# A megakernel of FFN, latent attention and FFN: moving the stages' transfers from SyncE's queue to ScalarE's

## The reference

```python
x = x + 0.5 * ffn(layernorm(x))        # x @ W.T + b, plus top-2 of 8 gated LoRA experts of rank 16
x = x + attention(layernorm(x))        # 16 heads, causal, 1024 tokens
x = x + 0.5 * ffn(layernorm(x))

# attention(x)
kv = rmsnorm(x @ W_kv) * g_kv          # rank 64
qc = x @ W_q                           # rank 128
q  = [qc @ W_qdec, rope(qc @ W_qrope)] # 16 + 32 columns a head
k  = [kv @ W_kdec, rope(x @ W_krope)]
out = softmax(causal(q @ k.T / sqrt(48))) @ (kv @ W_vdec) @ W_o
```

## Time and profile before

| what | value |
|---|---|
| median of three | 1967.87 us |
| the profiled execution | 1969.61 us, span 1967.9 us |
| PE busy | 1883.3 us, 96% of the span |
| DVE, ACT, POOL busy | 1428.7, 1017.2, 854.4 us |
| mean granted TensorE clock | 0.978 |
| moved by DMA | 307.60 MB, mean 156 GB/s |

### The profile page before, as it was taken

One profiled execution on the slowest core, in us unless ns is written; L12 is line 12 of the kernel. 1 busy time (PEld: TensorE's weight loads), 2 busy tenths in 40 slices (PEclk: granted clock), 3 DMA queues, 4 the chain that ended last, 5 costly groups with the idle time before them and its releaser, 6 DMA issues.

```text
span 1967.9 us, 32231 instructions
## 1 busy us (share of the span) xinstructions
PE 1883.3 (96%) x10832; PEld 1313.5 (67%) x10832; DVE 1428.7 (73%) x4570; ACT 1017.2 (52%) x2125; POOL 854.4 (43%) x912
## 2 busy tenths in 40 slices
PE   6789999999999999999999999999999999999994
PEld 5446666767776676767767777667767677677653
DVE  5667777777777787777877777777777778677622
ACT  3335555555555555555554555555555545555550
POOL 3456454443545445355443545444453544522121
PEclk9789999999999999999999999999999999999997
DMA  3675675676775667666675676656677666665511
GB/s 103 190 184 158 164 191 152 155 186 167 172 178 131 177 155 184 167 159 158 162 177 146 162 199 158 158 156 161 159 175 192 152 146 178 174 154 121 113 33 46
DMA packets 169813, 307.60 MB, mean 156 GB/s; under 512 B 15088, under 2 KB 33776, under 8 KB 169648
## 3 DMA queue, kind: packets, MB, share of 16 engines
q1 hardware_dynamic: 169648, 305.53, 61.7%
HBM read 179.12 MB, written 126.35 MB: 155 GB/s over the span
## 4 chain that ended last, share of the span: by engine, by line
PE 81%; DVE 7%; DMA 6%; ACT 2%; issue 2%; POOL 1%; SPq 1%; POOLq 0%; DVEq 0%
PE mx_b L788 14%; PE st_b L756 14%; PE st_b L758 12%; PE o_b L776 12%; PE tp_b L824 5%; DMA st<-k_scratch 4%; PE tp_b L821 4%; PE wj_b L713 4%; PE wj_b L700 3%; PE wj_b L682 3%; PE wj_b L693 2%; PE wj_b L715 2%; DVE mx_b L975 1%; PE wj_b L722 1%; PE wj_b L728 1%
## 5 line engine op out<-in xcount | busy, mean ns | idle before, releaser
L861 ACT ACTIVATE probs<-st_b 128x512 f32<-128x512 f32 (+3 forms) x1536 | 700.4, 489 | 569.3 <-PE st_b L758 519.5
L975 DVE CUSTOM_DVE_ANT_0 mx_b<-mx_b,tri 128x256 f32<-128x256 f32 (+3 forms) x1024 | 511.0, 515 | 118.9 <-PE mx_b L788 114.7
L756 PE MATMUL st_b<-st 97*128 97x512 f32 (+2 forms) x1536 | 578.7, 381 | 7.1 <-ACT probs L861 4.7
L788 PE MATMUL mx_b<-st 96*128 96x256 f32 (+2 forms) x1536 | 554.3, 406 | 19.2 <-DVE mx_s L975 8.1
L758 PE MATMUL st_b<-st,k_st 96*128 96x512 f32 (+2 forms) x1536 | 531.8, 350 | 0.0
L978 DVE TENSOR_REDUCE mx_s<-mx_b 128x1 f32<-128x512 f32 (+1 forms) x512 | 333.8, 652 | 137.3 <-PE mx_b L788 132.0
L788 PEld LDWEIGHTS mx_b<-st 96*128 96x128 f32 x1536 | 279.6, 192 | 203.7 <-issue 107.3
L1176 POOL TENSOR_SCALAR_AFFINE_SELECT probs<-probs 128x512 f32<-128x512 f32 x256 | 166.7, 658 | 529.7 <-ACT probs L861 529.7
L756 PEld LDWEIGHTS st_b<-st 97*128 97x128 f32 x1536 | 291.9, 190 | 105.5 <-ACT probs L861 39.8
L758 PEld LDWEIGHTS st_b<-st,k_st 96*128 96x128 f32 x1536 | 294.2, 192 | 30.1 <-issue 9.1
L776 PE MATMUL o_b<-probs,v_s 128*17 128x512 f32 (+3 forms) x3072 | 287.2, 492 | 0.9 <-POOL probs L1176 0.9
(11 more groups left out here) (192 smaller groups left out, 2281.6 us busy)
## 6 DMA issues: line engine op xcount, KB each, us to landing
st<-q_scratch SPq DMA_DIRECT2D x128, 384.0 KB, 5.8
st<-k_scratch SPq DMA_DIRECT2D x128, 384.0 KB, 8.6
k_st<-k_scratch SPq DMA_DIRECT2D x128, 384.0 KB, 8.7
q_scratch<-hi_t SPq DMA_DIRECT2D x32, 768.0 KB, 4.3
q_scratch<-lo_t SPq DMA_DIRECT2D x32, 768.0 KB, 5.3
k_scratch<-hi_t SPq DMA_DIRECT2D x30, 768.0 KB, 6.2
k_scratch<-lo_t SPq DMA_DIRECT2D x30, 768.0 KB, 4.8
ao_scratch<-o_f SPq DMA_DIRECT2D x256, 32.0 KB, 1.9
```

What stands on the lines that cost most here:

```text
L756: nc.tensor.matmul(dst, k1_st[u][0:SHIFT + 1, a, P * j:P * j + P], q_st[u][0:SHIFT + 1, a, q0:q0 + w], start=True, stop=False)
L788: nc.tensor.matmul(mx_b[:, m % 2, 0:w], q_st[u][0:SHIFT, a, P * i:P * i + P], k1_st[u][0:SHIFT, a, k0:k0 + w], start=True, stop=True).then ...
L861: nc.scalar.activation(probs[:, a, PLACE[s]:PLACE[s] + n], st_b[:, a % 2, HALF - n:HALF], ACT.Exp, scale=SCALE).then_inc(exp_done, 1)
L975: nc.vector.tensor_tensor_reduce(src, src, tri[:, HALF - n:HALF], 1.0, NEG, ALU.add, ALU.max, dst).then_inc(mx_done, 1)
```

## The change

ACT's queue now issues the stages' transfers (letters D and d, 80 steps with the same waits as before), the eleven weight transfers, and the stores of the high parts (u, 64). SP keeps the stores of the low parts (u, 64), the stacks, the shift rows and the attention output: 384 letters. All five order strings are new; PE, DVE and POOL have the same letters as before in another order, and ACT has 144 more.

```diff
-SP_STEPS = {JOB_A: ("x_load", "x_store"), JOB_C: ("x_load", "ao_load", "x_store")}
+LOADS = {JOB_A: ("x_load", "x_store"), JOB_C: ("x_load", "ao_load", "x_store")}
     "ACT": {
+        "D": [(name, n) for n in range(NJ) if LANE[n] == 0 for name in LOADS[JOBS[n][0]]],
+        "d": [(name, n) for n in range(NJ) if LANE[n] == 1 for name in LOADS[JOBS[n][0]]],
+        "u": [("store", n, 0) for n in range(NU)],
     "SP": {
-        "u": [("store", n, hl) for n in range(NU) for hl in range(2)],
+        "u": [("store", n, 1) for n in range(NU)],
-        "J": [(name, n) for n in range(NJ) if LANE[n] == 0 for name in SP_STEPS[JOBS[n][0]]],
-        "j": [(name, n) for n in range(NJ) if LANE[n] == 1 for name in SP_STEPS[JOBS[n][0]]],
@@ scalar
+                elif name == "x_load":
+                    if done:
+                        act.wait_ge(own.stored, 16 * done)
+                        if JOBS[own_last][0] == JOB_A:
+                            act.wait_ge(own.normed[1], count(own_last, 1) + 1)
...
+                    nc.scalar.dma_start(own.xa[:, :, :], x_g[k] if kind == JOB_A else x1_d[k]).then_inc(own.x_in, 16)
+                    if n == 0:
+                        load_first()
+                    elif n == 1:
+                        load_attention()
+                elif name == "ao_load":
...
+                elif name == "x_store":
+                    act.wait_ge(own.wj_free, bank_use(n, "y1") + 1)
+                    nc.scalar.dma_start(x1_d[k] if kind == JOB_A else out_g[k], own.xa[:, :, :]).then_inc(own.stored, 16)
+                elif name == "store":
+                    act.wait_ge(hic_done, n + 1)
+                    act.wait_ge(hir_done, n + 1)
+                    scratch_free(act, n)
+                    nc.scalar.dma_start(scratch_rows(n, 0), hl_t[SPARE[n]][0][:, :, :].bitcast(F32)).then_inc(
+                        hl_out[SPARE[n]][0], 16)
```

`scratch_free` and `scratch_rows` are new names for lines 616 to 621 before, unchanged. The strings, cut to their heads (whole ones have 3892, 2107 or 2251, and 528 or 384 letters):

```diff
 PE
-"JJJJPPPPjjjjJJJjjjJJJJPjjPjPJjPPPPPJPJJjPJPPXXPXPXXXPXXJXPXJXXPJXXPXXPFPXXXXXXXXXPXXPJXJXXSSXXSSXXSSPXXS..."
+"JJJJPPPPjjjjJJJjjjJJJJPjjPjPJjPPPPPJPJJjPJPPXXPPXXXPXXPXXJPXXJXXPJXXPXPXXXXXXXXXFXPXXJJPXXXXXXXXXXSXSXPX..."
 ACT
-"BJJJJwwwwwCCCJCjjjjJjjJJJJCjjCjCJjCHCCHCCJCJJjCJJCHCHCCCJCCBCCHCCCEEEEEEHEEEEECCEECEEEHCCCJJJEEEHEJCEECE..."
+"DBdJJJJwwwwwCCCJCjjjjJjjDDdJJJJCjjCjCJjCHCuCHuCCJCJJjCJJCHCuHuCCCCJCBCDCHuCCDCHEEuECEECEECEEEEEEEEHEuCCC..."
 SP
-"JjJJjuuuuquuuukqqsusuquukJuusJasssuuuuqksusqauksusuaJJqkususqakuussauuqkuqsaksusJsuuaqkJJsqsakssuuaqkuuJ..."
+"uuqkuuqqqsuskuussassuqkuqsksaussuaqkuqskasussauqkusqsakussaqkusqskaussaqkuqsaksussaqkqsksuassaqkuqsksuas..."
```

More of the change, by code:

```diff
@@ L238 @@
+        "MnJMMJMMoMMoMoMoMJMJJJJJMMJMMfJMJnJMMoMoMoMMoJMMJMMMMMMMMMMMMMMMJMMJMMJMMJfJnMMMMJMMJMMoMMooMoMMMJJJJJMM"
+        "JMMfJMnMJJoJMMoMoMMoJMMJMMMMMMMMMMMMMMMMMMMMMfnMMMMMMMoooMMoMMMMMMMfnMMMMMooMoMMoMMMMMMMMMMMMMMMMMMMMMMM"
         "MfnooooooooJJJJJJJJJJJJJJJJJJJoooojjjjjjjjjjjjjjjjjjj",
@@ L530, in rope, with scratch_free, scratch_rows @@
             engine.tensor_tensor(r[:, 1, :], r[:, 1, :], r[:, 0, :], ALU.add).then_inc(roped[SPARE[n]], 1)
+        def scratch_free(engine, n):
+            m, pair, side = UNIT[n]
+            b, half = divmod(m, 2)
+            if b > 1:
+                g = NQ * (b - 2) + NQ // NP * (pair + 1) - 1
+                engine.wait_ge(qk_in[g % 2][half], 64 * (g // 2 + 1))
+                engine.wait_ge(k2_in[half], 32 * (g + 1))
+        def scratch_rows(n, hl):
+            m, pair, side = UNIT[n]
+            b, half = divmod(m, 2)
+            rows = qk_d[side][b % 2, hl, PH * DQ * pair:PH * DQ * (pair + 1), HALF * half:HALF * (half + 1)]
+            return rows.rearrange("(r x) t -> r x t", x=3)
         def landed(sp, g, half):
@@ L562, in _ @@
-            for name, n, *arg in walk("SP"):
-                if name == "x_load":
-                    kind, k = JOBS[n]
-                    own = lanes[LANE[n]]
-                    done = IN_LANE[n]
-                    if done:
-                        own_last = max(i for i in range(n) if LANE[i] == LANE[n])
-                        sp.wait_ge(own.stored, 16 * done)
-                        if JOBS[own_last][0] == JOB_A:
-                            sp.wait_ge(own.normed[1], count(own_last, 1) + 1)
-                    if kind == JOB_C:
-                        before = JOB_OF[JOB_A, k]
-                        sp.wait_ge(lanes[LANE[before]].stored, 16 * (IN_LANE[before] + 1))
-                    if done and LANE[n]:
-                        sp.wait_ge(pv_done, NV * QUADS)
-                    sp.dma_start(own.xa[:, :, :], x_g[k] if kind == JOB_A else x1_d[k]).then_inc(own.x_in, 16)
-                    if n == 0:
-                        load_first()
-                    elif n == 1:
-                        load_attention()
-                elif name == "ao_load":
-                    k = JOBS[n][1]
-                    own = lanes[LANE[n]]
-                    b, half = divmod(k, 2)
-                    sp.wait_ge(ao_out, 64 * (2 * (NQ * b + NQ - 1) + half + 1))
-                    if LANE[n]:
-                        sp.wait_ge(pv_done, NV * QUADS)
-                    else:
-                        earlier = [i for i in range(n) if LANE[i] == LANE[n] and JOBS[i][0] == JOB_C]
-                        if earlier:
-                            sp.wait_ge(own.wj_full, bank_use(earlier[-1], "wo1") + 1)
-                    sp.dma_start(own.aoc[:, :, :], ao_d[b].rearrange("(k p) t -> p k t", p=P)[
-                        :, :, GT * P * half:GT * P * (half + 1)]).then_inc(own.ao_in, 16)
-                elif name == "x_store":
-                    kind, k = JOBS[n]
-                    own = lanes[LANE[n]]
-                    sp.wait_ge(own.wj_free, bank_use(n, "y1") + 1)
-                    sp.dma_start(x1_d[k] if kind == JOB_A else out_g[k], own.xa[:, :, :]).then_inc(own.stored, 16)
-                elif name == "store":
-                    hl = arg[0]
-                    m, pair, side = UNIT[n]
-                    b, half = divmod(m, 2)
-                    if hl:
-                        sp.wait_ge(lor_done, n + 1)
-                    else:
-                        sp.wait_ge(hic_done, n + 1)
-                        sp.wait_ge(hir_done, n + 1)
-                    if b > 1:
-                        g = NQ * (b - 2) + NQ // NP * (pair + 1) - 1
-                        sp.wait_ge(qk_in[g % 2][half], 64 * (g // 2 + 1))
-                        sp.wait_ge(k2_in[half], 32 * (g + 1))
-                    rows = qk_d[side][b % 2, hl, PH * DQ * pair:PH * DQ * (pair + 1), HALF * half:HALF * (half + 1)]
-                    sp.dma_start(rows.rearrange("(r x) t -> r x t", x=3),
-                                 hl_t[SPARE[n]][hl][:, :, :].bitcast(F32)).then_inc(hl_out[SPARE[n]][hl], 16)
@@ L616, in _ @@
+            for name, n, *arg in walk("SP"):
+                if name == "store":
+                    sp.wait_ge(lor_done, n + 1)
+                    scratch_free(sp, n)
+                    sp.dma_start(scratch_rows(n, 1), hl_t[SPARE[n]][1][:, :, :].bitcast(F32)).then_inc(
+                        hl_out[SPARE[n]][1], 16)
                 elif name == "qk":
@@ L919, in _ @@
                                          ACT.Copy).then_inc(tp_free, 1)
+                elif name == "x_load":
+                    kind, k = JOBS[n]
+                    own = lanes[LANE[n]]
+                    done = IN_LANE[n]
+                    if done:
+                        own_last = max(i for i in range(n) if LANE[i] == LANE[n])
+                        act.wait_ge(own.stored, 16 * done)
+                        if JOBS[own_last][0] == JOB_A:
+                            act.wait_ge(own.normed[1], count(own_last, 1) + 1)
+                    if kind == JOB_C:
+                        before = JOB_OF[JOB_A, k]
+                        act.wait_ge(lanes[LANE[before]].stored, 16 * (IN_LANE[before] + 1))
+                    if done and LANE[n]:
+                        act.wait_ge(pv_done, NV * QUADS)
+                    nc.scalar.dma_start(own.xa[:, :, :], x_g[k] if kind == JOB_A else x1_d[k]).then_inc(own.x_in, 16)
[4 more added lines that the diff above has]
+                elif name == "ao_load":
+                    k = JOBS[n][1]
+                    own = lanes[LANE[n]]
+                    b, half = divmod(k, 2)
+                    act.wait_ge(ao_out, 64 * (2 * (NQ * b + NQ - 1) + half + 1))
+                    if LANE[n]:
+                        act.wait_ge(pv_done, NV * QUADS)
+                    else:
+                        earlier = [i for i in range(n) if LANE[i] == LANE[n] and JOBS[i][0] == JOB_C]
+                        if earlier:
+                            act.wait_ge(own.wj_full, bank_use(earlier[-1], "wo1") + 1)
+                    nc.scalar.dma_start(own.aoc[:, :, :], ao_d[b].rearrange("(k p) t -> p k t", p=P)[
+                        :, :, GT * P * half:GT * P * (half + 1)]).then_inc(own.ao_in, 16)
+                elif name == "x_store":
```

(4 more changed lines are left out.)

216 lines of the change are left out of this document (107 added, 109 removed).

## The result

The changed kernel takes 1991.42 us (median of 4 runs, 1989.92 to 1993.81); the kernel before, in runs beside it, 1968.65 (1966.32 to 1969.46). The ratio is 1.0115, with a 95% interval of 1.0095 to 1.0136. The forecast was 1968.6 us and no change: it was wrong by 23 us, and the time lies outside its range.

What follows compares the result with a forecast made beforehand. The prediction took PE, busy 96% of the span, to bound the kernel. Its terms, -2 + 0.1 + 0.6 + 3 + 1 - 2 = +0.7 us, gave a median of 1968.6 us, no measurable change; range 1954 to 1984 us.

Steps and rivals of the forecast that it cites:

- Bound: Whole span: PE bounds, busy 96%; SP is often blocked and PE hardly notices.
- The stacks: SP's queue: stacks no longer held behind stages and high parts; -2 us, ends -6.9 and 0.
- The first loads: Kernel start, now issued by ACT: +0.1 us if its queue issues without pause; ends 0 and +5.
- Store of job 1 ahead of the evacuations: Opening: ACT issues this store right before job 0's four evacuations, delaying the opening's chain; +0.6 us.
- ACT issues in the body: 128 transfers between ACT's first and last exponential make exponentials late for PE; +3 us, ends 0 and 58.
- Loads right behind stores: ACT stands at job loads until the lane's store lands, at jobs 28 to 29 and 29 to 30; +1 us, ends 0 and +4.
- The order strings: Body counts alike, tail unchanged, opening differs and fills PE's idle time; -2 us, ends -10 and +5.
- ACT's issues reach PE: Rival, body: issues hold ACT's string, exponentials come late and PE's scores wait; 1980 us, chance 0.22.
- Nothing gets earlier: Rival: DMA engines limit the stacks, a second queue only interleaves; stack and opening gains vanish; 1972.6 us, chance 0.07.
- The opening: Rival, 50 to 150 us: freed stages and first units shrink PE's idle time and half-clock pieces; about 1957 us, chance 0.31.
- The signs: Changed profile if right: PE busy within 3 us of 1883, small stack and exponential waits, late job 0 evacuation, unchanged last 50 us.

Runs made afterwards that it cites:

- E2: Kernel before with its old order strings; stage transfers and high stores moved from SyncE's into ScalarE's string: 1969.28 us, ratio 1.0005.
- after: The changed kernel itself, with new order strings and new queues: 1991.42 us, ratio 1.0115 to the kernel before.
- E4: Changed kernel with only the jobs' loads and stores and the first loads put back into SyncE's string; high stores stay with ScalarE: 1994.39 us, ratio 1.0129.
- E10: Changed kernel, strings untouched; first lane's jobs before attention keep x in its own place, so its load needn't wait for the preceding store: 1984.54 us, ratio 1.0084.
- E6: Changed kernel with job 28 reading the attention output of two jobs before, loaded about 18 us earlier: 1982.89 us, ratio 1.0071.
- E9: New order strings up to score 540 (about 764 us), old ones from there, on all engines, with the new queues: 1974.49 us, ratio 1.0032.
- E11: E10 and E6 together: x in its own place and job 28's attention output taken from two jobs before: 1977.3 us, ratio 1.0048.
- E1: Changed kernel's new strings with every stage transfer and high store put back from ScalarE's into SyncE's string: 2001.16 us, ratio 1.017.
- E8: E2's kernel with the x loads of the ten even jobs 8 to 26 four or five letters later in ScalarE's string: 2000.2 us, ratio 1.0161.
- E5: Changed kernel with statistics and normalisation of x for seven jobs 1 to 4 letters later in VectorE's string: 2014.25 us, ratio 1.0223.
- E15: Changed kernel with quad 29's first-half stack loads held on SyncE until job 28's attention output has landed: 1988.46 us, ratio 1.0108.

## Why the prediction was wrong

*Bound.* Right: TensorE bounds, and its idle time decides.

*The stacks.* Forecast -2 us. TensorE's waits for stacks from 200 to 1850 us fell from 2.8 to 1.3, but 1.7 for shift rows came. SP is blocked as much as ever: its stack loads now wait 347.5 us for exponentials, its low stores 374.4 for VectorE, instead of the waits of the earlier trace rows. With the old strings (E2) nothing was gained.

```profile
SPq L566 <- DVE lo_t L1040: 374.4, 48, 58.3
SPq L577 <- ACT probs L830: 347.5, 47, 20.1
```

*The first loads.* Forecast +0.1, the queue issuing beside the instruction. Right: all nine further transfers go out from 3.05 to 8.31 us, beside the table load and the row of ones (ScalarE and its queue):

```profile
2.98 1.28 ACT L865 ACT_TABLE_LOAD   x1 [2.98 <-issue]
3.05 0.39 ACTq L903 DMA_DIRECT2D probs<-in_x  x1
...
4.28 3.61 ACT L865 ACTIVATE st<-ones 1x4096 fp32r<-1x4096 f32 x1
...
7.58 0.73 ACTq L811 DMA_DIRECT2D lo_t<-in_sin  x1
```

*Store of job 1 ahead of the evacuations.* Forecast +0.6. They start at 40.77 us, 0.8 later than in the earlier trace rows. Right as to the place; whether it is still in the total, no run shows.

*ACT issues in the body.* Forecast +3, bounds 0 and 58. Right in size: E2 has the same 144 letters in ScalarE's string, at the places that the old order gives them, and costs 1 us in sum. (The 0.33 to 0.45 us for an issue left out the 0.50 and 1.19 of the same rows; that changed only the upper bound.) In after ScalarE stood 15 us at open waits for a store's landing, and TensorE's waits for exponentials grew by 5.0 us; but that comes with the new strings, and in E4, without it, the time is no better.

*Loads right behind stores.* Forecast +1, for jobs 28 to 29 and 29 to 30. There nothing grew: 2.95 and 2.96 us from store to load. The place was the other kind of pair, a job behind attention and the one after it, which I had put down as having four letters or more, hence safe. I measured distance in letters on ScalarE and not what the landing of a store takes beside a high store (7.4 us at job 9), nor that VectorE's statistics follow 8 us behind the store.

*The order strings.* Forecast -2, bounds -10 and +5; measured +22 with the new queues (1.0115 less E2's 1.0005). This is the step that failed, in sign and in bounds. I took the body as equal because counts of letter pairs were alike (381 changes against 373), and looked for a difference only in the opening. Counts say nothing of how far a consumer stands behind the transfer that feeds it. What the runs put in their place: some 6 us for the chain of x (E10), 9 for job 28's attention output (E6), 6 for the first part of the strings (E9, not taken apart), which is 21 of 22 to 23 us. As single measurements of 2 us or more uncertainty each these don't exclude an overlap: E11 joins two of them and leaves 9 us. That the strings cost this is shown; what the first part's 6 us are stays open.

*The rivals.* "ACT's issues reach PE" gave the nearest time, 1980 us, and has the wrong cause: with no issue on ScalarE at all the new strings are slower still (E1). "Nothing gets earlier" is what the new queues alone do (E2). The opening did not tighten. The sentence on what would make the forecast wrong altogether, new strings that fit the chip's real durations worse, is what happened; I gave it no chance and no width of its own, and should have.

*The signs.* Most of what was to show the forecast right came true: TensorE waits 2.2 us for stacks (under 5) and 6.9 for exponentials from 200 to 1850 us (under 8; it is 9.2 over the whole span), job 0's evacuation stands at 40.77 us (40.6 or later), and the last stretch is as before. PE's busy time missed its 3 us by one. None of these signs looks at the attention output or at VectorE's waits for x, so they could not tell this outcome from the forecast's.

## What to carry to other kernels

Where a change comes with newly made order tables, treat the tables as a change of their own, and give them the widest bound in the sum; the first experiment is the old order with the new mechanism and the reverse. To compare two orders, list for every transfer the time from its issue to its first use in the old trace, beside what it takes to land there, and look in the new order for uses that have come nearer: of the 35 us by which E8 lengthened ten chains of the old order 31 were paid; but a wait can also be covered, as E10's last 8.0 us were. Moving the consumer later is no cure when its own consumer is as near (E5); a place of its own for the data won 6 us in the new order, and nothing in the old.

## What was not expected of the hardware

A load of 512 KB took 11.2 us to land beside stack loads of 384 KB each, with a median of 4.3, and 3.8 us with these held back (E15); a store of the same size took 7.4 us beside a store of 768 KB. The Trainium skill (DMA: Bandwidth & Descriptors, section "Issuing engines are not separate DMA queues") says that all issuers share the 16 DMA engines; the trace agrees: the stack loads, issued from SP's queue, slowed the load issued from ScalarE's. In E1, all on one queue, job 28's wait was 5.9 us, nearly as long. Three more of the fifteen such loads in after took 10.1, 10.4 and 13.0 us, and TensorE waited for none of them: a slow landing costs only where the first use is near.

A kernel's single executions, with the same strings, drift by up to 5 us on the way (the middle part cost 3.1 to 8.5 us in seven of them), while many stretches of 48 scores between are alike to 0.1 us: I take what varies to be where transfers land, which no run here isolates; a wait of that kind should be priced from more than one trace.
